# A 12-stage decoder on one core: layer norms' moments taken in the stage before, weight sums and GpSimd fills moved, and another order in the second state-space layer

## The chip, the cores and the metric

The kernel runs on one core of a Trainium2 chip. The metric is the device time of one execution in microseconds (us). Before the change three runs gave a median of 2445.35 us (2441.73 to 2446.42).

## What is computed

The input is `x` of 4 batches x 256 tokens x 256 features in fp32, with a context and two side inputs. The reference is a pre-norm decoder of four layers with three sublayers each:

```python
h = _layernorm(x)                 # mean and variance over the 256 features, eps 1e-5
x = x + sublayer(h)               # twelve times, each with another sublayer
```

The sublayers that the text speaks of, with the short names that the kernel's tiles carry:

- l1a: causal attention with an output bias; m1a and m1b: a Mamba layer (input product, convolution over 4 tokens, SiLU, a product down to 40 rows, a product from 8 of them up again, softplus, then the scan); l1f: a linear layer with ternary weights, added to `x`
- l2a: rotary attention; l2x: experts with quantised weights; l2f: a router keeps the 128 best of 256 tokens of a batch, and only these get the output of a two-layer GELU network
- l3s to l3e: a state-space layer of 16 blocks of 128 channels whose output passes a layer norm with `gamma` and `beta` and then `W_out`; l3xa: cross attention with positions and an output bias; l3f: top-4 of 8 experts

Inside the third layer's state-space part, `layernorm(y) * gamma + beta` times `W_out` is computed as `y @ (gamma * W_out)`, minus the mean times the column sums of `gamma * W_out`, plus the column sums of `beta * W_out`.

## The kernel before

The 1024 tokens lie in 8 tiles of 128 (`NT = 8`, two tiles of one batch, `ST = 2`). The residual `res`, the normed `xn` and its transpose `xT` stay in SBUF for the whole kernel. A stage is a `Stage` block; its exit is a barrier of all engines. In a stage each engine runs its own program in written order, and semaphores alone tie the engines to one another.

Every sublayer but the first begins with `normalize` (tiles `ln_*`; ln4 is the norm ahead of sublayer 4, m1a). It is a `Stage` of its own. SyncE starts the sublayer's weight loads and waits for them. VectorE takes `bn_stats` of eight tiles (L237), `bn_aggr` of them (L241), adds eps (L249, "guess"), refines with a Newton step what ScalarE's Ln and Exp give (L254, L260, L266), makes `shift` (L272) and two normed tiles of each half (L277); ScalarE makes the other four. TensorE transposes, VectorE (L308, L310) and ScalarE (L338, L340) copy to `xT`. ScalarE loads the Exp/Ln table set at the stage's start (L324). GpSimd fills `rowsL` and `rowsR` with ones in ln9 (L320, `ones_in`).

- `attend` (l1a, l2a, l3xa) goes head by head through 4 batches. TensorE's scores `pA` (L1601) wait until VectorE has reduced an earlier `pA` to its maxima (`maximum`, L1734). Four heads make a quad, which VectorE divides by its sum (L1742, L1744). Once a batch, `residual(u)` adds the projected output to `res` (L1779, or L1781 and L1782 with a bias).
- m1a works on two halves of the tokens. `conv`, `silu` (L2031) and the scan's inputs are VectorE's; TensorE makes `pd` (40 rows, L1957) and, from ScalarE's copy of it (`xd`, L1993), the delta product (L1962); ScalarE makes the sigmoids (L1987) and the softplus in four passes (L1997 to L2006).
- l1f: TensorE's products are added by VectorE, a tile at a time (L2242).
- l2x: GpSimd adds the first batches' outputs to `res`; VectorE unscales each (L2644) and adds the last.
- l2f: TensorE makes the up products (L2355), ScalarE the GELU, and the down products (L2366, tile by tile, three PSUM buffers, each freed by VectorE's L2410). VectorE adds the bias (L2410) and the kept tokens to `res` (L2413). It also prepares l3: `scale_and_sum` scales a row block of `W_out` by `gamma` and adds up the sums (L2314, L2316, L2318): 16 blocks, eight of them ahead of the down products and two ahead of each of the first four tiles.
- l3s (`mamba3_ends` with `end=None`) makes the first inputs (`px`, L3175) and from the sums the constants `gw` (two products, a copy L3232). l3e is its counterpart at the end (`start=None`): VectorE adds `gw` to `res` (L3209) and then waits for TensorE's out projection (L3212).

## Time and profile before

| | |
|---|---|
| median of 3 runs | 2445.35 us |
| profiled execution, its own time | 2442.86 us |
| its span | 2441.0 us |
| mean granted TensorE clock | 0.864 of 2.4 GHz |
| busy: TensorE, VectorE, ScalarE, GpSimd | 81%, 72%, 55%, 17% |

The span is the time between the first and the last recorded instruction. Durations of the rows below are from this one execution. An engine's busy share is a mean over twelve sublayers with different limits, so a change in one of them is read from the rows there.

### The profile page before, as it was taken

How to read it: one execution, taken by the hardware profiler on the slowest of the kernel's cores; microseconds unless marked ns; L12 is line 12 of the kernel's file. 1: busy time of each engine (PE TensorE's matmuls, PEld its weight loads, DVE VectorE, ACT ScalarE, POOL GpSimd, SP SyncE). 2: the span in 40 equal slices, each digit the busy share in tenths (PEclk: the TensorE clock that was granted, in tenths of full speed). 3: DMA queues.
4: the chain of work that ended last, by engine and by line, in shares of the span. 5: the costliest groups of instructions: out<-in, count | busy, mean ns of one | idle time of the engine just before them, and what ended most of it. 6: DMA issues, size and time to landing. Idle time of an engine off the chain costs nothing. (4 is left out here: it accounts for less than half of the span.)

```text
span 2441.0 us, 34752 instructions
## 1 busy us (share of the span) xinstructions
PE 1988.1 (81%) x11321; PEld 1310.9 (54%) x11337; DVE 1754.3 (72%) x3900; ACT 1345.1 (55%) x2646; POOL 420.7 (17%) x585
## 2 busy tenths in 40 slices
PE   6999999987666666766877895597999999958978
PEld 4776767764333333543654353455766676733545
DVE  6878888777999998647785874674736373568734
ACT  5777777766989896254334365423323333352641
POOL 2333333322111110003532000201101010110000
PEclk8999999997877777786787798598999999976989
DMA  5000000002111102304202100150000000042010
GB/s 222 3 2 2 3 3 2 1 1 99 58 59 59 40 1 66 114 9 86 54 2 75 51 3 18 49 201 2 1 2 0 2 0 2 1 115 70 16 37 18
DMA packets 62030, 94.52 MB, mean 39 GB/s; under 512 B 9403, under 2 KB 48139, under 8 KB 59415
## 3 DMA queue, kind: packets, MB, share of 16 engines
q1 hardware_dynamic: 58604, 87.81, 11.4%
q0 software_dynamic: 1728, 4.22, 0.8%
q8 instruction: 82, 1.34, 0.2%
q10 hardware_dynamic: 1536, 0.49, 0.1%
q14 instruction: 80, 0.66, 0.1%
HBM read 80.53 MB, written 10.49 MB: 37 GB/s over the span
## 5 line engine op out<-in xcount | busy, mean ns | idle before, releaser
L1260 DVE SCALAR_TENSOR_TENSOR moe_acc<-moee_eo,moe_wsel,moe_acc 128x256 f32<-128x256 bf16 x512 | 226.0, 512 | 0.6
L867 DVE SCALAR_TENSOR_TENSOR l_acc<-l_px,l0w_chan,l_acc 128x253 f32<-128x253 f32 (+2 forms) x288 | 137.6, 478 | 80.6 <-POOL l_acc L835 80.1
L1192 ACT CAST moee_eo<-moee_po 128x512 bf16<-128x512 f32 x256 | 132.5, 596 | 38.5 <-PE moee_po L1165 33.8
L1165 PE MATMUL moee_po<-moee_db,moee_hb 96*128 96x256 bf16 (+1 forms) x768 | 126.9, 329 | 26.1 <-ACT moee_eo L1192 15.5
L1150 PE MATMUL moee_pu<-moe_xb,moee_wb 128*128 128x512 bf16 x192 | 73.1, 522 | 83.4 <-DVE moee_ub L1249 83.4
L1165 PEld LDWEIGHTS moee_po<-moee_db,moee_hb 96*128 96x128 bf16 (+1 forms) x768 | 87.6, 116 | 73.0 <-ACT moee_eo L1192 20.9
L1704 ACT ACTIVATE l3xa_ex<-l3xa_pS 128x512 f32<-128x512 f32 x128 | 74.2, 606 | 81.1 <-PE l3xa_pS L1617 76.7
L1704 ACT ACTIVATE l2a_ex<-l2a_pS 128x512 f32<-128x512 f32 x128 | 73.8, 606 | 76.7 <-PE l2a_pS L1617 72.2
L540 PE MATMUL l_pz<-xT,l0w_w_in 128*128 128x256 f32 x384 | 111.4, 414 | 2.5 <-DVE l_sz L915 2.5
L351 PE MATMUL ln_pt<-ident,xn 128*128 128x128 f32 x176 | 39.6, 418 | 85.9 <-DVE xn L277 85.9
L540 PE MATMUL l_px<-xT,l0w_w_in 128*128 128x256 f32 x384 | 103.5, 394 | 4.3 <-DVE l_acc L867 4.3
L3052 ACT COPY l3b_bc<-l3b_pbc 128x512 f32<-128x512 f32 x48 | 28.1, 586 | 136.4 <-PE l3b_pbc L3002 136.4
L2124 ACT ACTIVATE m1b_dA<-m1w_delta,m1w_a 128x255 f32<-128x255 f32 x128 | 53.3, 462 | 85.8 <-DVE m1b_h L2165 83.4
L652 PE MATMUL l_po<-l0w_w_out,l_yg 128*128 128x256 f32 x384 | 100.4, 385 | 0.0
L3002 PE MATMUL l3b_pbc<-l3w_xin,l3w_w_in 128*128 128x256 f32 x384 | 95.7, 393 | 5.3 <-PEq L72 5.3
L1734 DVE TENSOR_REDUCE l3xa_negm<-l3xa_pA 128x2 f32<-128x512 f32 x128 | 83.1, 684 | 22.8 <-PE l3xa_pA L1601 21.0
L1734 DVE TENSOR_REDUCE l2a_negm<-l2a_pA 128x2 f32<-128x512 f32 x128 | 82.9, 684 | 21.6 <-PE l2a_pA L1601 19.8
L698 ACT ACTIVATE l_acc<-l_px,l0w_chan 128x256 f32<-128x256 f32 x96 | 54.0, 563 | 78.7 <-PE l_px L540 78.5
L852 POOL TENSOR_TENSOR l_ssum<-l_ssum,l_sq 128x256 f32<-128x256 f32 x92 | 68.1, 741 | 148.0 <-ACT l_sq L742 148.0
L2214 PE MATMUL m1b_py<-m1b_hc,ident 128*128 128x256 f32 x256 | 77.3, 466 | 20.1 <-DVE m1b_y L2149 11.4
L903 DVE TENSOR_TENSOR l_gg<-l_dec,l_m 128x768 f32<-128x768 f32 x96 | 91.5, 953 | 0.2
L2135 POOL TENSOR_TENSOR m1b_dBu<-m1w_du,m1b_bc 128x1024 f32<-128x1024 f32 x32 | 75.2, 2354 | 93.9 <-DVE m1b_h L2165 51.9
(614 smaller groups left out, 5508.3 us busy)
## 6 DMA issues: line engine op xcount, KB each, us to landing
moe_wf<-in_moe_up SPq DMA_DIRECT2D x48, 256.0 KB, 2.8
l3w_w_in<-in_l_w_in SPq DMA_DIRECT2D x1, 8224.0 KB, 25.9
m1b_bc<-bc_rows SPq DMA_DIRECT2D x16, 512.0 KB, 10.4
moe_df<-in_moe_down SPq DMA_DIRECT2D x48, 128.0 KB, 3.2
l_qs<-parts_q SPq DMA_DIRECT2D x36, 128.0 KB
l0w_w_in<-in_l_w_in SPq DMA_DIRECT2D x2, 1536.0 KB, 12.7
l0w_w_out<-in_l_w_out SPq DMA_DIRECT2D x1, 3072.0 KB
parts_q<-l_pieces SPq DMA_DIRECT2D x16, 192.0 KB, 2.3
```

What stands on the lines that cost most here:

```text
L540: last = nc.tensor.matmul(out, w_in[:, k, c0:c0 + w], xT[:, k, b, :], start=(k == 0), stop=(k == KT - 1))
L652: last = nc.tensor.matmul(po[:, t * D:(t + 1) * D], yg[:, u % RY, t * P:(t + 1) * P], w_out[:, j, :], start=(j == 0 and t == 0), stop=(j = ...
L867: nc.vector.scalar_tensor_tensor(out=a, in0=px[:, 0:S - (L0_CONV - 1 - c)], scalar=w, in1=a, op0=ALU.mult, op1=ALU.add).then_inc(tap_done, 1)
L903: nc.vector.tensor_tensor(gg[:, :, :], dec[:, v % 2, :, :], m3[:, bv % 2, None, :].broadcast_to([P, 2, SC]), ALU.mult).then_inc(gg_done, 1)
L1165: last = nc.tensor.matmul(po[:, t, :], hb[rows, j % H, t * P:(t + 1) * P], db[rows, j % H, :], start=(n == 0), stop=(n == len(parts) - 1))
L1192: nc.scalar.copy(eo[:, e % 2, 2 * q:2 * q + 2, :], po[:, 2 * q:2 * q + 2, :]).then_inc(o_read, 1)
L1260: last = nc.vector.scalar_tensor_tensor(out=acc[:, t, :], in0=eo[:, e % 2, t, :], scalar=wsel[:, t, e:e + 1], in1=acc[:, t, :], op0=ALU.mu ...
L1704: nc.scalar.activation(ex[:, at % XR, :, :], pS[:, at % 2, :, :], ACT.Exp, scale=scale).then_inc(exp_done, 1)
L1734: nc.vector.tensor_reduce(negm[:, u % 2, t, 2 * pair:2 * pair + 2], pA[:, at % 2, :, 0:keys(t)], AX, ALU.max, negate=True).then_inc(maxed, 1)
L2135: nc.gpsimd.tensor_tensor(dBu[:, i % R, :, :], du[:, n, None, b * S:(b + 1) * S].broadcast_to([P, CH, S]), bc[:, b % 2, c * CH:(c + 1) * C ...
L2214: last = nc.tensor.matmul(py[:, n, :], g["ident"][:, :], hc[:, i % R, q, :], start=(c == 0 and n == 0 and q == 0), stop=(c == NCH - 1 and ...
L3002: last = nc.tensor.matmul(pbc[:, n * S:(n + 1) * S], w_in[:, k, c0 + j * P:c0 + (j + 1) * P], xin[:, k, :], start=(k == 0), stop=(k == KT ...
```

## The change

It has five parts.

1. `stats` and `mv` are tiles of the whole kernel. `moments_ahead` takes the moments of some tiles in the stage before the norm, on VectorE, as soon as their residual is final: 6 tiles for ln4, ln6, ln7, ln9, ln10 and ln11, 4 for ln8; ln1, ln2, ln3 and ln5 are as before. `normalize(..., ahead=n)` begins with "guess" of the first half and takes the moments of what is left. Its table load moves to the end of ScalarE's program of the stage before (for ln8 and ln10 it goes, as that set is loaded there).
2. `scale_and_sum` runs once per tile in l2f (blocks 0 to 7, none ahead of the tiles), and blocks 8 to 15 in l3s, where the two `gw` products move behind the `px` products.
3. GpSimd's two fills move from ln9 to the start of l2f.
4. m1a: on VectorE `silu(0)` stands ahead of `conv(1, 0)`; on ScalarE the first half's sigmoids stand ahead of the gate's, its `copy_xd(0)` ahead of the second half's sigmoids, and its first softplus ahead of `copy_xd(1)`.
5. The waits that go with these (`added`, `summed`, `out_chain`, `early_added`, `sums_done`).

```diff
-def normalize(nc, g, loads=(), early=None, ones_in=(), mix=None):
+def moments_ahead(nc, g, link, tiles):
+
+    for t in tiles:
+        last = nc.vector.bn_stats(g["stats"][:, t, :], g["res"][:, t, :])
+    link(last)
+    for t in tiles:
+        nc.vector.bn_aggr(g["mv"][:, t, :], g["stats"][:, t, :])
+
...
-                for t in range(H):
-                    stat(t)
-                stat(4)
-                for t in range(H):
-                    aggregate(t)
-                stat(5)
-                guess(0)
-                stat(6)
-                stat(7)
-                newton_a(0)
-                aggregate(4)
-                aggregate(5)
-                newton_b(0)
-                aggregate(6)
-                aggregate(7)
+                if ahead:
+                    guess(0)
+                    for t in range(ahead, NT):
+                        stat(t)
+                    newton_a(0)
+                    for t in range(ahead, NT - 1):
+                        aggregate(t)
+                    newton_b(0)
+                    aggregate(NT - 1)
+                else:
...
-                nc.scalar.preload_act_table_set(EXP_LN)
+                if not ahead:
+                    nc.scalar.preload_act_table_set(EXP_LN)
...
                         nc.scalar.copy(oT[:, :, :], pE[:, :].rearrange("p (k q) -> p k q", k=KT)).then_inc(oT_done, 1)
+                nc.scalar.preload_act_table_set(EXP_LN)
...
-                        residual(batch_at(j, ADD_AT))
+                        u = batch_at(j, ADD_AT)
+                        residual(u)
+                        if u < B - 1:
+                            dve.wait_ge(added, u + 1)
+                            moments_ahead(nc, g, link, range(ST * u, ST * (u + 1)))
...
                     nc.scalar.activation(gate[:, :, :], xn[:, :, :], ACT.Sigmoid).then_inc(gate_sig, 1)
-                    for half in range(2):
-                        for n in range(M1_ET):
-                            act.wait_ge(conv_done, M1_ET * half + n + 1)
-                            nc.scalar.activation(sig[:, n, tokens(half)], u[:, n, tokens(half)],
-                                                 ACT.Sigmoid).then_inc(sig_done, 1)
+                    copy_xd(0)
+                    sigmoid(1, 0)
+                    sigmoid(1, 1)
                     nc.scalar.preload_act_table_set(EXP_LN)
                     nc.scalar.activation(a[:, :, :], a[:, :, :], ACT.Exp).then_inc(exp_done, 1)
-                    for half in range(2):
-                        act.wait_ge(xd_proj, half + 1)
-                        nc.scalar.copy(xd[:, tokens(half)], pd[0:M1_R + 2 * M1_N, half, :]).then_inc(xd_done, 1)
...
+                    softplus(0, 0)
+                    copy_xd(1)
+                    softplus(0, 1)
+                    softplus(1, 0)
+                    softplus(1, 1)
...
                     conv(0, 0)
                     conv(0, 1)
+                    silu(0)
                     conv(1, 0)
-                    silu(0)
                     conv(1, 1)
                     silu(1)
...
                     for t in range(NT):
+                        if 1 <= t < NT - 1:
+                            dve.wait_ge(summed, t)
+                            moments_ahead(nc, g, link, (t - 1,))
                         dve.wait_ge(added, t + 1)
                         dve.wait_ge(outp, t + 1)
                         nc.vector.tensor_tensor(res[:, t, :], res[:, t, :], po[:, t % 4, 0:D], ALU.add).then_inc(summed, 1)
+
+                @block.scalar
+                def _(act):
+                    nc.scalar.preload_act_table_set(EXP_LN)
...
+                @block.gpsimd
+                def _(pool):
+                    for rows in ahead["rows"]:
+                        nc.gpsimd.memset(rows[:, :, :], 1.0)
...
+                    nc.scalar.preload_act_table_set(EXP_LN)
...
-                    for j in range(L3_J // 2):
-                        scale_and_sum(dve, link, j)
                     dve.wait_ge(second_in, 32)
                     for t in range(NT):
-                        for j in range(L3_J // 2 + 2 * t, min(L3_J // 2 + 2 * t + 2, L3_J)):
-                            scale_and_sum(dve, link, j)
+                        if t == 0:
+                            dve.wait_ge(ahead["out_in"], 32)
+                        scale_and_sum(nc, link, ahead, t)
+                        if 1 <= t < NT - 1:
+                            dve.wait_ge(out_chain, t)
+                            moments_ahead(nc, g, link, (t - 1,))
                         dve.wait_ge(down, t + 1)
...
                     unscale(6)
+                    dve.wait_ge(early_added, 2)
+                    moments_ahead(nc, g, link, range(0, 2 * ST))
                     unscale(7)
...
+        half_tokens(nc, g, {"w_in": w_in, "w_out": w_out, "chan": chan, "sums": sums, "w_in_in": w_in_in,
+                            "out_in": out_in, "rows": (rowsL, rowsR)})
         g["stage"] = 9
-        normalize(nc, g, early=(w_in_in, 16), ones_in=(rowsL, rowsR))
+        normalize(nc, g, early=(w_in_in, 16), ahead=6)
...
+                if end is None:
+                    pe.wait_ge(sums_done, 1)
+                    for n in range(2):
+                        last = nc.tensor.matmul(po[:, n, 0:D], g["ones"][:, 0:P], m["sums"][:, n, :], start=True,
+                                                stop=True)
+                    last.then_inc(gw_ready, 1)
...
                         link(nc.vector.tensor_tensor(now, now, gw[:, 1, :], ALU.add))
+                    if start is None:
+                        moments_ahead(nc, g, link, range(NT - ST))
                     dve.wait_ge(used, ST)
...
                 if end is None:
+                    for j in range(NT, L3_J - 1):
+                        scale_and_sum(nc, link, m, j)
+                    row = w_out[:, L3_J - 1, 0:D]
+                    link(nc.vector.scalar_tensor_tensor(out=m["sums"][:, 1, :], in0=row,
+                                                        scalar=m["chan"][:, L3_J - 1, 2:3], in1=m["sums"][:, 1, :],
+                                                        op0=ALU.mult, op1=ALU.add))
+                    link(nc.vector.tensor_scalar(row, row, m["chan"][:, L3_J - 1, 1:2], None, ALU.mult))
+                    nc.vector.tensor_tensor(m["sums"][:, 0, :], m["sums"][:, 0, :], row, ALU.add).then_inc(sums_done, 1)
                     dve.wait_ge(gw_ready, 1)
                     nc.vector.tensor_copy(gw[:, :, :], po[:, :, 0:D])
```

On VectorE in l2f, at the down products' second tile (`l2f_po` is their PSUM, `l3w_w_out` and `l3w_sums` are `W_out` and its sums for l3), before:

```order
L2410 TENSOR_TENSOR l2f_tmp<-l2f_po,l2fw_b 128x256
L2413 SCALAR_TENSOR_TENSOR res<-l2f_tmp,l2f_keep,res 128x256
L2314 SCALAR_TENSOR_TENSOR l3w_sums<-l3w_w_out,l3w_chan,l3w_sums 128x256
L2316 TENSOR_SCALAR l3w_w_out<-l3w_w_out,l3w_chan 128x256
L2318 TENSOR_TENSOR l3w_sums<-l3w_sums,l3w_w_out 128x256
L2314 SCALAR_TENSOR_TENSOR l3w_sums<-l3w_w_out,l3w_chan,l3w_sums 128x256
L2316 TENSOR_SCALAR l3w_w_out<-l3w_w_out,l3w_chan 128x256
L2318 TENSOR_TENSOR l3w_sums<-l3w_sums,l3w_w_out 128x256
L2410 TENSOR_TENSOR l2f_tmp<-l2f_po,l2fw_b 128x256
L2413 SCALAR_TENSOR_TENSOR res<-l2f_tmp,l2f_keep,res 128x256
```

and after:

```order
L2464 TENSOR_TENSOR l2f_tmp<-l2f_po,l2fw_b 128x256
L2467 SCALAR_TENSOR_TENSOR res<-l2f_tmp,l2f_keep,res 128x256
L2322 SCALAR_TENSOR_TENSOR l3w_sums<-l3w_w_out,l3w_chan,l3w_sums 128x256
L2324 TENSOR_SCALAR l3w_w_out<-l3w_w_out,l3w_chan 128x256
L2326 TENSOR_TENSOR l3w_sums<-l3w_w_out 128x256
L208 BN_STATS stats<-res 128x6
L211 BN_AGGR mv<-stats 128x2
L2464 TENSOR_TENSOR l2f_tmp<-l2f_po,l2fw_b 128x256
L2467 SCALAR_TENSOR_TENSOR res<-l2f_tmp,l2f_keep,res 128x256
```

One block of `W_out` stands ahead of the tile where two stood, and the moments of the tile before have come in.

On ScalarE at the middle of m1a (`m1a_sig` the sigmoids of two pieces a half, `m1w_gate` that of the gate, `m1w_xd` the copy of the 40 rows), before:

```order
L1980 COPY m1a_raw<-m1a_px 128x2x256 x4
L1983 ACT_TABLE_LOAD
L1983 ACTIVATE m1w_gate<-xn 128x2048
L1987 ACTIVATE m1a_sig<-m1w_u 128x512 x4
L1989 ACT_TABLE_LOAD
L1990 ACTIVATE m1w_a<-m1w_a 128x32
L1993 COPY m1w_xd<-m1a_pd 40x512
L1997 ACTIVATE m1a_soft<-m1a_px,m1w_chan 128x512
```

and after:

```order
L2006 COPY m1a_raw<-m1a_px 128x2x256 x4
L2012 ACT_TABLE_LOAD
L2012 ACTIVATE m1a_sig<-m1w_u 128x512 x2
L2036 ACTIVATE m1w_gate<-xn 128x2048
L2017 COPY m1w_xd<-m1a_pd 40x512
L2012 ACTIVATE m1a_sig<-m1w_u 128x512 x2
L2040 ACT_TABLE_LOAD
L2041 ACTIVATE m1w_a<-m1w_a 128x32
L2022 ACTIVATE m1a_soft<-m1a_px,m1w_chan 128x512
```

The first `m1w_xd` has moved ahead of two sigmoids, the table load and `m1w_a`.

On VectorE in l2a at the residual of the first batch (`l2a_pA` scores, `l2a_negm` their maxima), before:

```order
L1734 TENSOR_REDUCE l2a_negm<-l2a_pA 128x2 x3
L1779 TENSOR_TENSOR res<-res,l2a_pE 128x256 x2
L1734 TENSOR_REDUCE l2a_negm<-l2a_pA 128x2
L1742 RECIPROCAL l2a_rden<-l2a_pX 128x8
L1744 TENSOR_TENSOR l2a_o<-l2a_pX,l2a_rden 128x32 x2
```

and after:

```order
L1755 TENSOR_REDUCE l2a_negm<-l2a_pA 128x2 x3
L1800 TENSOR_TENSOR res<-res,l2a_pE 128x256 x2
L208 BN_STATS stats<-res 128x6 x2
L211 BN_AGGR mv<-stats 128x2 x2
L1755 TENSOR_REDUCE l2a_negm<-l2a_pA 128x2
L1763 RECIPROCAL l2a_rden<-l2a_pX 128x8
L1765 TENSOR_TENSOR l2a_o<-l2a_pX,l2a_rden 128x32 x2
```

Four operations stand between the add and the next reduction of scores.

## Rows read from the trace of the kernel before

**Rows 1.** The page: TensorE's granted clock in 40 slices of the span.

```profile
PEclk8999999997877777786787798598999999976989
```

**Rows 2.** Timeline of VectorE in ln7: start, us, then line, names, idle before.

```profile
1498.02 1.73 DVE L237 BATCH_NORM_STATS2 ln_stats<-res 128x6 f32<-128x256 f32 x5 [1.28 <-PEq L72]
...
1500.26 0.15 DVE L249 TENSOR_SCALAR ln_var<-ln_mv 128x4 f32<-128x4 f32 x1
...
1505.92 0.42 DVE L310 COPY xT<-ln_pt 128x256 f32<-128x256 f32 x1
```

**Rows 3.** SyncE's queue in ln7: what it waited for, us, times, longest.

```profile
SPq L222 <- PEq L222: 3.3, 1, 3.3
```

**Rows 4.** SyncE's queue in ln11, the same columns.

```profile
SPq L222 <- PEq L222: 0.2, 1, 0.2
```

**Rows 5.** Timeline of VectorE in ln9.

```profile
1660.11 2.40 DVE L249 TENSOR_SCALAR ln_var<-ln_mv 128x4 f32<-128x4 f32 x1
...
1666.64 0.41 DVE L310 COPY xT<-ln_pt 128x256 f32<-128x256 f32 x1
```

**Rows 6.** Timeline of GpSimd in ln9.

```profile
1655.51 3.50 POOL L320 MEMSET l3w_rowsL<- 38x4096 bf16 x1 [88.27 <-POOLq L72]
1658.96 3.52 POOL L320 MEMSET l3w_rowsR<- 38x4096 bf16 x1
```

**Rows 7.** Timeline of VectorE, its first operation in l2f.

```profile
1588.06 0.23 DVE L2386 TENSOR_SCALAR l2f_score<-l2f_ps,l2fw_b_r 128x8 f32<-128x8 f32 x1 [7.79 <-PE l2f_ps L2344]
```

**Rows 8.** Timeline of TensorE in l2f: where the down products resume.

```profile
1633.11 1.22 PE L2366 MATMUL l2f_po<-l2fw_w,l2f_hT 128*128 128x256 f32 x2 [4.54 <-DVE l2f_tmp L2410]
```

**Rows 9.** Timeline of VectorE in l2f's down products.

```profile
1631.26 0.48 DVE L2314 SCALAR_TENSOR_TENSOR l3w_sums<-l3w_w_out,l3w_chan,l3w_sums 128x256 f32<-128x256 f32 x1
...
1632.63 0.42 DVE L2410 TENSOR_TENSOR l2f_tmp<-l2f_po,l2fw_b 128x256 f32<-128x256 f32 x1
...
1649.93 0.42 DVE L2410 TENSOR_TENSOR l2f_tmp<-l2f_po,l2fw_b 128x256 f32<-128x256 f32 x1 [2.51 <-PE l2f_po L2366]
...
1653.39 0.42 DVE L2410 TENSOR_TENSOR l2f_tmp<-l2f_po,l2fw_b 128x256 f32<-128x256 f32 x1 [2.51 <-PE l2f_po L2366]
```

**Rows 10.** l2f in stretches: us, busy of each engine, granted clock, DMA share.

```profile
1633.10:1638.60 5.50, 5.49 (x13) 4.41 (x14) 5.15 (x13) 0.00 (x0) 0.00 (x0) 0.50 0.01 3
```

**Rows 11.** Timeline of TensorE in l3s.

```profile
1671.40 14.58 PE L3175 MATMUL l3s_px<-l3w_w_in,l3w_xin 128*128 128x512 f32 x32
```

**Rows 12.** Timeline of VectorE in m1a, the second half's first convolution.

```profile
1097.67 2.33 DVE L2020 SCALAR_TENSOR_TENSOR m1w_u<-m1a_raw,m1w_chan,m1w_u 128x512 f32<-128x512 f32 x3
```

**Rows 13.** Timeline of TensorE in m1a.

```profile
1101.25 3.63 PE L1957 MATMUL m1a_pd<-m1w_u,m1w_w_x 128*40 128x512 f32 x4 [7.02 <-DVE m1w_u L2031]
1106.74 3.78 PE L1962 MATMUL m1a_px<-m1w_xd,m1w_w_dt 8*128 8x512 f32 x4 [1.86 <-ACT m1w_xd L1993]
```

**Rows 14.** Timeline of ScalarE in m1a.

```profile
1114.12 0.58 ACT L1993 COPY m1w_xd<-m1a_pd 40x512 f32<-40x512 f32 x1
1116.86 0.69 ACT L1997 ACTIVATE m1a_soft<-m1a_px,m1w_chan 128x512 f32<-128x512 f32 x1 [2.16 <-PE m1a_px L1962]
...
1121.46 0.63 ACT L2006 ACTIVATE m1a_soft<-m1a_soft 128x512 f32<-128x512 f32 x1
```

**Rows 15.** Timeline of VectorE in l2a, at the first residual add.

```profile
1411.76 0.74 DVE L1779 TENSOR_TENSOR res<-res,l2a_pE 128x256 f32<-128x256 f32 x2
```

**Rows 16.** Timeline of TensorE in l2a behind that add.

```profile
1414.19 0.39 PE L1601 MATMUL l2a_pA<-l_ks,l_qs 96*128 96x256 bf16 x2
```

**Rows 17.** Timeline of TensorE in l3xa behind the first residual add.

```profile
2272.77 0.39 PE L1601 MATMUL l3xa_pA<-l3x_ks,l3x_qs 96*128 96x256 bf16 x2 [0.54 <-DVE l3xa_negm L1734]
```

**Rows 18.** Timeline of VectorE in l1f's adds.

```profile
1291.62 0.42 DVE L2242 TENSOR_TENSOR res<-res,l1f_po 128x256 f32<-128x256 f32 x1 [0.44 <-PE l1f_po L2255]
```

**Rows 19.** Timeline of VectorE in l2x, the last tile.

```profile
1568.85 0.88 DVE L2644 SCALAR_TENSOR_TENSOR l2x_h<-l2x_po,l2x_rows,l2x_wrow 128x256 f32<-128x256 f32 x2 [2.96 <-PE l2x_po L2867]
```

**Rows 20.** Timeline of VectorE in l3e.

```profile
2139.51 0.16 DVE L3212 TENSOR_SCALAR l3e_small<-l3e_po 128x2 f32<-128x2 f32 x1 [15.40 <-PE l3e_pq L3162]
```

More of the change, by code:

```diff
@@ L239, in aggregate @@
                 def aggregate(t):
-                    dve.wait_ge(stats_done, t + 1)
+                    dve.wait_ge(stats_done, t + 1 - ahead)
                     nc.vector.bn_aggr(mv[:, t, :], stats[:, t, :]).then_inc(moments, 1)
@@ L246, in guess @@
                 def guess(h):
-                    dve.wait_ge(moments, (h + 1) * H)
+                    if (h + 1) * H > ahead:
+                        dve.wait_ge(moments, (h + 1) * H - ahead)
                     nc.vector.tensor_scalar(var[:, half(h)], mv[:, half(h), 1], LN_EPS, None,
@@ L278, in scaled @@
                                             ALU.subtract, ALU.mult).then_inc(xn_v, 1)
-                for t in range(H):
-                    stat(t)
-                stat(4)
-                for t in range(H):
-                    aggregate(t)
-                stat(5)
-                guess(0)
-                stat(6)
-                stat(7)
-                newton_a(0)
-                aggregate(4)
-                aggregate(5)
-                newton_b(0)
-                aggregate(6)
-                aggregate(7)
+                if ahead:
[8 more added lines that the diff above has]
+                else:
+                    for t in range(H):
+                        stat(t)
+                    stat(4)
+                    for t in range(H):
+                        aggregate(t)
+                    stat(5)
+                    guess(0)
+                    stat(6)
+                    stat(7)
+                    newton_a(0)
+                    aggregate(4)
+                    aggregate(5)
+                    newton_b(0)
+                    aggregate(6)
+                    aggregate(7)
                 newton_c(0)
@@ L1853, in positional_cross @@
         vaug = st.sbuf("vaug", [P, NT, H, HD + 1])
-        normalize(nc, g, [(w[:, :, :, :], I["l3x_w"]), (wk[:, :, :, :], I["l3x_wk"]), (rows[:, :], I["l3x_row"])])
+        normalize(nc, g, [(w[:, :, :, :], I["l3x_w"]), (wk[:, :, :, :], I["l3x_wk"]), (rows[:, :], I["l3x_row"])],
+                  ahead=6)
         stacks = head_stacks(st, H, H)
@@ new lines, in copy_xd, with softplus @@
+                    def copy_xd(half):
+                        act.wait_ge(xd_proj, half + 1)
+                        nc.scalar.copy(xd[:, tokens(half)], pd[0:M1_R + 2 * M1_N, half, :]).then_inc(xd_done, 1)
+                    def softplus(half, n):
+                        i = M1_ET * half + n
+                        act.wait_ge(dt_proj, i + 1)
+                        nc.scalar.activation(soft[:, 0, n, tokens(half)], px[:, n, half, :],
+                                             ACT.Identity, bias=chan[:, n, 5:6]).then_inc(a_chain, 1)
+                        act.wait_ge(a_chain, 3 * i + 1)
+                        nc.scalar.activation(soft[:, 1, n, tokens(half)], soft[:, 0, n, tokens(half)],
+                                             ACT.Abs).then_inc(a_chain, 1)
+                        act.wait_ge(a_chain, 3 * i + 2)
+                        nc.scalar.activation(soft[:, 2, n, tokens(half)], soft[:, 1, n, tokens(half)], ACT.Exp,
+                                             scale=-1.0).then_inc(a_chain, 1)
+                        act.wait_ge(a_chain, 3 * i + 3)
+                        nc.scalar.activation(soft[:, 3, n, tokens(half)], soft[:, 2, n, tokens(half)], ACT.Ln,
+                                             bias=1.0).then_inc(soft_done, 1)
@@ L2264, with scale_and_sum @@
 MOD_KEEP = S // 2
+def scale_and_sum(nc, link, m, j):
+    w_out, sums, gamma, beta = m["w_out"], m["sums"], m["chan"][:, j, 1:2], m["chan"][:, j, 2:3]
+    row = w_out[:, j, 0:D]
+    if j == 0:
+        nc.vector.memset(w_out[:, :, D:D + 1], 1.0)
+        link(nc.vector.tensor_scalar(sums[:, 1, :], row, beta, None, ALU.mult))
+        link(nc.vector.tensor_scalar(row, row, gamma, None, ALU.mult))
+        return
+    link(nc.vector.scalar_tensor_tensor(out=sums[:, 1, :], in0=row, scalar=beta, in1=sums[:, 1, :],
+                                        op0=ALU.mult, op1=ALU.add))
+    link(nc.vector.tensor_scalar(row, row, gamma, None, ALU.mult))
+    before = w_out[:, 0, 0:D] if j == 1 else sums[:, 0, :]
+    link(nc.vector.tensor_tensor(sums[:, 0, :], before, row, ALU.add))
 def half_tokens(nc, g, ahead):
@@ L2294, in half_tokens @@
             rope = g["xn"][:, :, :].rearrange("p (n t) d -> p n (t d)", n=2)
[L2295 removed]
+            w_out, chan = ahead["w_out"], ahead["chan"]
             ph = st.psum("ph", [P, 4, 512])
@@ L2545, in quant_experts @@
         wgu = wst.sbuf("wgu", [P, KT, B, S])
-        normalize(nc, g, [(wgu[:, :, :, :], I["l2x_gu"])])
+        normalize(nc, g, [(wgu[:, :, :, :], I["l2x_gu"])], ahead=6)
         with Stage(nc, "l2x") as st:
@@ L3163, in _ @@
                                          start=True, stop=True).then_inc(used, 1)
-                if end is None:
-                    for n in range(2):
-                        last = nc.tensor.matmul(po[:, n, 0:D], g["ones"][:, 0:P], m["sums"][:, n, :], start=True,
-                                                stop=True)
-                    last.then_inc(gw_ready, 1)
                 if start is not None:
```

63 lines of the change are left out of this document (21 added, 42 removed).

## The prediction

> **What bounds the kernel now.** The page comes first: TensorE is busy for 81% of the span, and its clock line [rows 1] stays below 9 over long stretches, so the stages have different limits. The change touches four kinds of places, so each is read from its own timeline, not from the shares. In a norm nothing else runs, and the path is a chain: VectorE's moments, the guess, ScalarE's Ln and Exp, Newton, the normed tiles, transposes, copies. In ln7 the statistics start at 1498.02, the guess comes at 1500.26, the last copy ends at 1506.34: 8.32 us [rows 2]. The other chain there is SyncE's, the weight loads; its queue's waits tell which of the two ends a norm. In ln7 SyncE waits 3.3 us for TensorE after its load has landed, so compute decides [rows 3]; in ln11 it waits only 0.2 us, so there the 2 MB of expert weights decide nearly as much [rows 4]. In l2f's down products TensorE stood idle for 4.54 us until VectorE had freed a buffer at L2410 [rows 8]. In m1a the engines hand one value back and forth, and TensorE waits 7.02 us for `silu` and 1.86 us for a copy on ScalarE [rows 13]. In l2a TensorE is paced by its own work, with VectorE just behind it [rows 15, 16].
>
> **The norms.** The moments of six tiles leave each of ln4, ln6, ln7, ln9, ln10, so the guess is the first operation: 1500.26 - 1498.02 = 2.24 us earlier [rows 2]. What follows keeps its spacing, since only two `bn_stats` (five took 1.73, so 0.35 each) still stand behind the guess and ScalarE needs about as long. I take 2.24 for each, 11.2 in all. Bounds: nothing, where SyncE ends the norm, and 2.24. SyncE's slack in ln7 is 3.3 [rows 3], and I take the others as ln7, their loads being of its kind; ln9 has no load. ln11 can give only its slack of 0.2 [rows 4]. ln8 has four tiles left, two more `bn_stats` between guess and Newton: 2.24 - 0.7 = 1.5. Sum: -12.9. The table load that went to the end of the stage before costs nothing there: ScalarE's last copies end ahead of VectorE's last adds, and if one didn't, a load would cost less than the 2.24 us of moments under which it lay in the norm.
>
> **The fills.** In ln9 the second L249 takes 2.40 us where such an operation takes 0.15 [rows 2, 5]; it ends at 1662.51, when the second fill has ended at 1658.96 + 3.52 = 1662.48 [rows 6]. From the first fill's start to VectorE's last copy the norm takes 1667.05 - 1655.51 = 11.5 us, in ln7 8.3 [rows 2, 5, 6]. So without the fills it gains 3.2: -3.2 (bounds 0 and 3.3). In l2f they lie where VectorE waits 7.79 us for the router's products, until 1588.06 [rows 7]; the fills take 7.02 [rows 6] from the stage's start, so they just fit: 0, at worst a few tenths. The Trainium skill (SBUF — State Buffer, "Who interferes with whom") says that VectorE and GpSimd share one pair of ports as an exclusive lock, and that a `tensor_scalar` in a two-port mode waits for a whole GpSimd instruction; by that rule the gain is the whole remainder of each fill, as the trace shows. The page would also let the fills hold l2f's first VectorE operations if they came later than that idle time.
>
> **l2f's down products.** Before, eight blocks of `W_out` and two more ahead of the first tile stand in front of VectorE's first L2410, which comes at 1632.63; a block takes 1632.63 - 1631.26 = 1.37 us [rows 9]. TensorE had filled its three buffers by 1633.11 - 4.54 = 1628.57, waited, and then ran at half clock for 5.5 us [rows 8, 10]; the last product ended at 1653.35 [rows 9]. Afterwards VectorE needs per tile 1.37 for a block, 0.5 for the moments (0.35 plus the aggregation) and 0.9 for the two old operations, 2.8 us, less than the 3.46 us that TensorE takes for a tile (1653.39 - 1649.93 [rows 9]). So TensorE isn't held: the remaining five tiles follow 1628.57 directly and end at 1628.57 + 5 x 3.46 = 1645.9. That is -7.5: 4.5 of idle time and 3 of half clock. Bounds: -4.5, if the clock falls there anyway; none, if `W_out` landed late, but its blocks were being worked on long before.
>
> l3s gets eight blocks, 8 x 1.37 = 11 us, under the 14.58 us of `px` [rows 11]. The two `gw` products move from in front of `px` to behind it, which is neutral, and the copy of `gw` now follows at the very end, where ScalarE's copy of the last `px` ended before: +0.2 (0 to 0.7).
>
> **m1a.** Before: `pd` of the first half starts at 1101.25 and takes 3.63, its copy waits on ScalarE behind a sigmoid and the table load, and the delta product starts at 1106.74 and ends at 1110.5 [rows 13]; then `pd` of the second half (another 3.6), its copy at 1114.12, the delta product, and two softplus from 1116.86 to 1122.09, 2.62 each [rows 14]. Afterwards `silu(0)` comes one `conv` (three passes in 2.33 us and a first one, together some 2.8 [rows 12]) earlier: it is done at about 1098.6, `pd` ends 1102.3, the copy (0.58) follows at once, the delta product ends 1106.7, the second `pd` 1110.4, its copy 1111.0. ScalarE has done one softplus by then, and three remain: 1111.0 + 3 x 2.62 = 1118.9 against 1122.09. So -3.0 (0.2 held back for hand-overs). Bounds: -4 if the clock opens earlier, -1 if the gate's sigmoid gets in front of the copy.
>
> **What it costs: attention.** Six tiles' moments stand in `attend` at u = 0, 1, 2 in l1a, l2a and l3xa: two `bn_stats` 0.7, a wait, two aggregations, 1.04 us in front of the next reduction (an estimate from [rows 2]). What is late next is that reduction, and then TensorE's `pA`. In l2a the `pA` product at 1414.19 starts as soon as the reduction behind the add (1411.76) and its followers allow [rows 15, 16]; in l3xa TensorE already waits 0.54 there [rows 17]. So the delay passes through whole at u = 0 and 1: 4 x 1.04 = 4.1. At u = 2 VectorE has idle time ahead of its next work, 0 to 0.3. l1a's quads are shorter on VectorE, and I take 1.0, 0.6 and 0.35: 2.0. Sum +6.1, bounds 0 and 9 x 1.04 = 9.4.
>
> The other moments are covered. l1f: the block (0.5) is a little longer than VectorE's wait of 0.44 per tile [rows 18]; that drifts for five tiles, and the last tile, with no block ahead of it, takes it back: +0.1 (without that, 0.5). l2x: four tiles, 1.8 us, in a wait of 2.96 [rows 19]. l3e: six tiles in 15.40 [rows 20].
>
> **The sum.** -12.9 - 3.2 - 7.5 - 3.0 + 6.1 + 0.2 + 0.1 = -20.2 us. Against the profiled execution's own 2442.86 us (span 2441.0 and 1.9 around it) that is 2422.7; the runs' median 2445.35 lies 2.5 above that execution, so 2425.2.
>
> **Rivals.** A measurement of this kernel tells about 0.2%, 4.9 us, from no change.
> - Attention pays nothing, since later slack takes the delays back: -26, 2419. For it: TensorE's path in l1a has waits of its own. Against: [rows 16, 17].
> - l2f gives only its idle time, because VectorE's chain or the late half clock paces it: 3 to 5 us less, 2429. Against: 2.8 under 3.46.
> - Attention pays double: each late reduction also delays ScalarE's exponentials and the next quad, or u = 2 costs as much: +6 more, 2431.
> - Slower: the stalls bring down TensorE's clock. After l2f's 4.54 us of idle time the clock was 0.50 for 5.5 us [rows 8, 10], which costs 2.75. If each of the nine stalls in attention did that: +24.8, 2450, slower than before. It decides from the point where a stall of 1 us is enough and does it at all nine. Against: the waits of l3xa [rows 17] leave the clock line at 9 in the slice that holds them (2258 to 2319) [rows 1]. [...]
> - The change doesn't shorten the norms: the loads, or ScalarE's table, end them, as in ln11. Then 12.7 of the gain are gone: -7.5, 2438, and with any further loss no change. Against: [rows 3].
>
> **Chances.** My forecast, -16 to -24, 0.65; attention free 0.10; l2f small 0.10; attention double 0.07; norms unchanged 0.05, of which half within 0.2%; slower by the clock 0.03. Faster 0.94, same 0.03, slower 0.03. The range leaves out the last two and the ends of the first: 2417 to 2434.
>
> **What would show it.** Right: in ln4, ln6, ln7, ln9, ln10 the guess first on VectorE and the norm 2.2 us shorter; ln9's L258 at 0.15; ln11 about as long as before, with SyncE's last wait for TensorE near 0; no idle time of TensorE over 1 us in l2f's down products, and a full clock there; m1a's last softplus ending 3 us sooner after the barrier ahead of m1a; behind each residual of l2a and l3xa at u = 0, 1 a wait of TensorE for `negm` of about 1 us. Wrong: norms that end on SyncE, a clock of 0.5 in attention, or a VectorE that waits at l2f's start for the fills.

## The result and the profile after

The changed kernel takes 2424.76 us (median of 4 runs, 2420.86 to 2426.5) against 2445.89 us for the kernel before with its runs of the same day (4 runs, 2441.73 to 2446.63). The ratio is 0.9917, its 95% interval 0.9901 to 0.9932, that is 16.6 to 24.2 us less. The forecast was 2425.2 us, within 2417 to 2434. The profiled execution has a span of 2419.0 us, 22.0 less than before. In the timelines below a line's columns are its start and duration in us, the engine, the line of kernel.py, the operation, the tiles written and read, their shapes, how many were merged, and in brackets the idle time before it with what ended it.

Norm ln7 on VectorE after the change, which answers to [rows 2]:

```profile
1493.04 0.17 DVE L258 TENSOR_SCALAR ln_var<-mv 128x4 f32<-128x4 f32 x1 [1.28 <-PEq L72]
1493.12 0.75 DVE L245 BATCH_NORM_STATS2 stats<-res 128x6 f32<-128x256 f32 x2
...
1498.81 0.42 DVE L329 COPY xT<-ln_pt 128x256 f32<-128x256 f32 x1
```

The guess comes first and the last copy ends 6.19 us after it, where it ended 8.32 us after the first statistics. In ln9, which answers to [rows 5], the second guess takes 0.17 and not 2.40 us, and the norm 6.31 us in all:

```profile
1637.73 0.17 DVE L258 TENSOR_SCALAR ln_var<-mv 128x4 f32<-128x4 f32 x1 [1.22 <-PEq L72]
...
1638.94 0.17 DVE L258 TENSOR_SCALAR ln_var<-mv 128x4 f32<-128x4 f32 x1
...
1643.62 0.42 DVE L329 COPY xT<-ln_pt 128x256 f32<-128x256 f32 x1 [0.16 <-PE ln_pt L371]
```

SyncE's queue in ln11 (what it waited for, total us, times, longest) says what it said in [rows 4]: the load ends the norm, and SyncE then waits only 0.2 us for TensorE:

```profile
SPq L230 <- DMA l3fw_w<-in_l3f_w: 7.0, 1, 7.0
...
SPq L230 <- PEq L230: 0.2, 1, 0.2
```

In l2f the fills lie where [rows 7] had the wait (first GpSimd, then VectorE); VectorE's first operation starts 1.3 us before the second fill ends (1579.02):

```profile
1572.06 3.50 POOL L2419 MEMSET l3w_rowsL<- 38x4096 bf16 x1 [12.04 <-POOLq L72]
1575.51 3.51 POOL L2419 MEMSET l3w_rowsR<- 38x4096 bf16 x1
```

```profile
1577.73 0.23 DVE L2438 TENSOR_SCALAR l2f_score<-l2f_ps,l2fw_b_r 128x8 f32<-128x8 f32 x1 [6.43 <-PE l2f_ps L2390]
```

Its matrix operand lies in PSUM and has 8 columns, and it wasn't held. The down products, which answer to [rows 8], are one group of 128 without a wait:

```profile
1607.57 27.89 PE L2412 MATMUL l2f_po<-l2fw_w,l2f_hT 128*128 128x256 f32 x128 [0.78 <-ACT l2f_hT L2426]
```

TensorE in m1a, for [rows 13]: the copy comes at once (0.67 and not 1.86 us of waiting), and ScalarE's last softplus ends 28.96 us after the stage's first operation, where it ended 33.46 us after it:

```profile
1098.00 2.54 PE L1983 MATMUL m1a_pd<-m1w_u,m1w_w_x 128*40 128x512 f32 x4 [4.16 <-DVE m1w_u L2070]
1101.21 3.78 PE L1988 MATMUL m1a_px<-m1w_xd,m1w_w_dt 8*128 8x512 f32 x4 [0.67 <-ACT m1w_xd L2017]
1105.03 3.64 PE L1983 MATMUL m1a_pd<-m1w_u,m1w_w_x 128*40 128x512 f32 x4
1109.33 1.99 PE L1988 MATMUL m1a_px<-m1w_xd,m1w_w_dt 8*128 8x512 f32 x4 [0.67 <-ACT m1w_xd L2017]
```

What it costs shows in l2a at the first residual, on VectorE and on TensorE [rows 15, 16]:

```profile
1404.71 0.74 DVE L1800 TENSOR_TENSOR res<-res,l2a_pE 128x256 f32<-128x256 f32 x2
1405.49 0.75 DVE L208 BATCH_NORM_STATS2 stats<-res 128x6 f32<-128x256 f32 x2
1406.28 0.25 DVE L211 BATCH_NORM_AGGREGATE mv<-stats 128x2 f32<-128x6 f32 x2
1406.44 0.66 DVE L1755 TENSOR_REDUCE l2a_negm<-l2a_pA 128x2 f32<-128x512 f32 x1
```

```profile
1407.16 0.39 PE L1621 MATMUL l2a_pA<-l_ks,l_qs 96*128 96x256 bf16 x2 [0.67 <-DVE l2a_negm L1755]
...
1408.19 0.39 PE L1621 MATMUL l2a_pA<-l_ks,l_qs 96*128 96x256 bf16 x2 [0.42 <-DVE l2a_negm L1755]
```

The reduction starts 1.73 us after the add did, where it started 0.66 after it (1412.42 against 1411.76), so a block costs 1.07; TensorE waits 0.67 and 0.42, together the same 1.09.

### The profile page after: what moved, and what is told of

Same layout as the page of the kernel before. It is cut to its first block and busy times, and to the rows that moved or that the text cites. A ratio compares the mean times of both kernels' runs of the same rounds, so it can differ in the third digit from the quotient of the medians.

```text
span 2419.0 us, 34769 instructions
## 1 busy us (share of the span) xinstructions
PE 1999.5 (83%) x11337; PEld 1312.5 (54%) x11337; DVE 1755.9 (73%) x3900; ACT 1344.7 (56%) x2644; POOL 421.3 (17%) x585
## 5 line engine op out<-in xcount | busy, mean ns | idle before, releaser
L1185 PE MATMUL moee_po<-moee_db,moee_hb 96*128 96x256 bf16 (+1 forms) x768 | 134.9, 343 | 28.4 <-ACT moee_eo L1212 21.0
L1212 ACT CAST moee_eo<-moee_po 128x512 bf16<-128x512 f32 x256 | 133.1, 595 | 38.3 <-PE moee_po L1185 35.5
L3131 POOL TENSOR_TENSOR l3w_yz<-l3b_ys,l3b_sz 128x256 f32<-128x256 f32 x48 | 40.1, 836 | 290.7 <-DVE l3b_ys L3160 290.7
```

The source lines that it names most:

```text
L1185: last = nc.tensor.matmul(po[:, t, :], hb[rows, j % H, t * P:(t + 1) * P], db[rows, j % H, :], start=(n == 0), stop=(n == len(parts) - 1))
L1212: nc.scalar.copy(eo[:, e % 2, 2 * q:2 * q + 2, :], po[:, 2 * q:2 * q + 2, :]).then_inc(o_read, 1)
```

## The experiments

There were eleven runs: the changed kernel and the kernel before once more, and nine variants. The medians of the kernel before lie between 2442.5 and 2446.0 us from run to run and its single executions up to 14 us apart, so the tables below go by stages of the profiled executions: a stage's length is from the first operation behind its opening barrier to the first one behind the next, read from the timelines. For attention TensorE's busy time in that window is given too. What is left, length less busy time, is its waiting, and that repeats within 0.1 us in kernels that share the code of l2a. The scatter lies in the busy time, which holds what the clock costs.

**Another execution of each kernel.**

> The changed kernel once more, for how far stages that no edit touches differ between executions. My theory: stages outside the change, and the pieces at half clock within it (the start of l2f, m1a's two pd products), move by 1 to 3 us from execution to execution, so that of m1a's 4.5 us measured only 3 are the edit's and of l2f's 8.9 only 7.5. Then m1a lasts 31.2 to 32.7 us here and l2f 65.7 to 67. Rival: the edits give the whole 4.5 and 8.9; then this execution repeats 31.2 and 65.7 within 0.1. Total 2421 to 2427 us by both.

2424.62 us (4 runs, 2422.23 to 2432.56), ratio 0.992 (0.9904 to 0.9935); but the profiled execution has a span of 2430.2, 11 us above the first. m1a took 31.16 and l2f 67.10. So of l2f's 8.8 us between the first two profiles 1.4 were scatter, and m1a's length repeated: the first theory holds for l2f, the rival for m1a as far as this run goes.

> The kernel before once more, for its stages. If m1a's 35.7 us in the first profile is a matter of where the clock stood, it takes 32.7 here, as in the three kernels that leave m1a alone; rival: it is the usual length, 35.7 again. l2f 73.2 to 74.5, ln9 12.3, l2a 157.7 to 158.6 by both.

2449.37 us (one execution). m1a took 34.62, l2f 73.21, ln9 12.31, l2a 158.52. m1a's 35.7 was neither the usual length nor a single case.

**The weight sums alone.** Edit: part 2 of the change in the kernel before, no moments moved.

```diff
-                    for j in range(L3_J // 2):
-                        scale_and_sum(dve, link, j)
...
                     for t in range(NT):
-                        for j in range(L3_J // 2 + 2 * t, min(L3_J // 2 + 2 * t + 2, L3_J)):
-                            scale_and_sum(dve, link, j)
...
+                        scale_and_sum(nc, link, ahead, t)
```

> The kernel before with the weight sums' move alone: one block per tile in l2f, eight in l3s, the gw products behind px; no moments moved. My theory: TensorE's idle time of 4.54 us and its 5.5 us at half clock both go, so l2f lasts 74.5 - 7.5 = 67.0 us (66 to 68 with the clock's scatter in its first products), and the kernel 7.3 us less than before. Rival: the half clock comes anyway (from where it falls in the run): l2f 70, kernel 4.3 less.

l2f took 67.03 us, l3s 19.85 (as before). Ratio 0.9965 (0.9945 to 0.9985), median 2434.25. The first theory.

**The same with the eight blocks ahead of the down products.**

```diff
                     for j in range(L3_J // 2):
-                        scale_and_sum(dve, link, j)
+                        scale_and_sum(nc, link, ahead, j)
...
                     for t in range(NT):
-                        for j in range(L3_J // 2 + 2 * t, min(L3_J // 2 + 2 * t + 2, L3_J)):
-                            scale_and_sum(dve, link, j)
```

> As the weight sums' move alone, but the eight blocks of l2f all stand ahead of the down products, as before. VectorE reaches the first bias add at about 1630.4 - not 1632.6 - so TensorE idles some 1.9 us and not 4.54. This asks what a shorter wait does to the clock. My theory (the half clock follows the long idle time): with 1.9 us of idle time no half clock, l2f 74.5 - 2.7 - 2.75 = 69 us. Rival, any wait of TensorE brings the half clock: l2f 71.8 us with a stretch of 0.50 behind the wait.

l2f took 69.06 us; ratio 0.9968 (0.9952 to 0.9983), median 2439.09. TensorE's timeline and the stretch behind the wait (length, busy of each engine, granted clock 1.00):

```profile
1628.53 11.71 PE L2366 MATMUL l2f_po<-l2fw_w,l2f_hT 128*128 128x256 f32 x53 [1.80 <-DVE l2f_tmp L2409]
```

```profile
1628.50:1634.00 5.50, 5.47 (x25) 4.85 (x26) 3.03 (x7) 0.00 (x0) 0.00 (x0) 1.00 0.04 13
```

The first theory. A wait of 1.80 us left the clock at 1.00 (2.4 GHz) here, one of 4.54 us was followed by 0.50 (1.2 GHz) [rows 8, 10], in all four executions profiled with it. So what l2f gains is the wait and its consequence, and the two don't shrink together: shortening the wait to 1.80 removed the half clock whole.

**m1a's order alone.** Edit: part 4 of the change in the kernel before.

> The kernel before with m1a's new order alone. My theory: m1a goes from 35.7 to 32.7 us with the clock where it was, and down to 31.2 where the first pd product meets the higher clock (it took 2.54 us and not 3.63 in the changed kernel). Rival: the whole 4.5 us is the order's; then 31.2 whatever that product takes. The kernel as a whole 3 us less than before.

m1a took 31.37 us. Ratio 0.9969 (0.9949 to 0.9988), median 2438.97. All lengths of m1a, over every profile:

| m1a | executions | us |
|---|---|---|
| order of before | 5 | 35.71, 34.62, 32.72, 32.73, 32.72 (mean 33.7) |
| order of after | 8 | 31.21, 31.16, 31.24, 31.26, 31.37, 30.23, 30.27, 30.26 (mean 30.9) |

The two groups don't overlap, and their means are 2.8 apart. Neither side of the expectation was right as put: the length is the order's and the clock's. Against the three executions of 32.7, the three of 30.2 are 2.5 less.

**The fills alone.** Edit: part 3 in the kernel before.

> The kernel before with GpSimd's two fills in l2f and no longer in ln9. My theory: they held VectorE in ln9; ln9 goes from 12.3 to 9.1 us (start to the next stage's first copy), l2f keeps 74.5, and the kernel is 3.2 us less. Rival: VectorE was slow there for another cause, as GpSimd's start or the weights' arrival: ln9 keeps over 11 us.

ln9 took 9.38 us and not 12.31, l2f 73.19. Ratio 0.9996 (0.9985 to 1.0008): 2.9 us in one stage aren't told from nothing by whole runs, the stage shows them.

**Attention without the moments.** ln4, ln7 and ln11 take all eight tiles themselves and load their table set themselves:

```diff
                         residual(u)
-                        if u < B - 1:
-                            dve.wait_ge(added, u + 1)
-                            moments_ahead(nc, g, link, range(ST * u, ST * (u + 1)))
```

> The changed kernel without the moments in attention: ln4, ln7 and ln11 take all eight tiles' moments themselves, with their table load. My theory: attention's blocks cost what the profile after shows, 2.9 us in l1a, 2.1 in l2a, 2.2 in l3xa, and the three norms give back 2.2, 2.1 and nothing; so this kernel is 2.8 us faster than the changed one (about 2422), l2a lasts 157.7 us and not 159.8, l3xa 161.1 and not 163.3, l1a 95.7 and not 98.6. Rival: attention's lengths differ for other causes (clock); then l2a and l3xa keep 159.8 and 163.3 and the kernel is 4.3 us slower than the changed one.

2423.85 us (6 runs), ratio 0.9919 (0.9905 to 0.9934): 0.8 less than the changed kernel where 2.8 was expected; whole runs tell neither of the two from nothing. l1a 93.53, l2a 160.40, l3xa 162.70, ln4 and ln7 9.37 and 9.32. By its length alone l2a would speak for the rival; the table below shows that its waiting is back at 19.06 and that the rest is 2.7 us of busy time. The clock stood at 0.50 for the stage's first 38.6 us, where it did for 35.6 with the changed kernel, and for 3.4 us more near its end.

**The moments in one block.** The same six tiles, but ahead of the last residual, where VectorE waits for the out projection:

```diff
+                        if u == B - 1:
+                            dve.wait_ge(added, B - 1)
+                            moments_ahead(nc, g, link, range(ST * (B - 1)))
                         residual(u)
-                        if u < B - 1:
-                            dve.wait_ge(added, u + 1)
-                            moments_ahead(nc, g, link, range(ST * u, ST * (u + 1)))
```

> The changed kernel with the six tiles' moments of each attention in one block ahead of the last residual, where VectorE waits 3.3 us or more for the out projection; a block of six takes about 2.9 us. My theory: a block costs only where VectorE is late next, so here nothing: l2a 157.7, l3xa 161.1, l1a 95.5 to 96; ln4 and ln7 stay at 7.1 and 7.0 us; the kernel is 6 to 7 us faster than the changed one, about 2418. Rival: the block doesn't fit and delays the last add by up to 2 us in each of the three; then 0 to 2 us faster than the changed one.

2417.4 us (6 runs, 2414.25 to 2423.8), ratio 0.9899 (0.9883 to 0.9915). l1a 95.39, l2a 158.63, l3xa 161.11, ln4 7.07, ln7 6.95. The first theory: in l2a VectorE waited 3.42 us ahead of the last add in the kernel before and 0.91 here. Not all of the 7.3 us that this kernel is faster by the medians is the block's, though: l3xp, the projections ahead of l3xa, which this edit doesn't touch, took 41.7 us here and in the kernel with both improvements, and 43.5 to 45.2 in the eleven other executions. TensorE's clock was 1.00 in its first 4 us in these two, and 0.50 for the first 3.4 us or more in the others. Why isn't known.

**The blocks doubled.**

```diff
                             moments_ahead(nc, g, link, range(ST * u, ST * (u + 1)))
+                            n = NT * ("l1a", "l2a", "l3xa").index(name)
+                            for t in range(ST * u, ST * (u + 1)):
+                                last = nc.vector.bn_stats(g["stats2"][:, n + t, :], g["res"][:, t, :])
+                            link(last)
+                            for t in range(ST * u, ST * (u + 1)):
+                                nc.vector.bn_aggr(g["mv2"][:, n + t, :], g["stats2"][:, n + t, :])
...
```

> The changed kernel with each of attention's nine blocks of moments taken twice (the second into tiles that nobody reads), so that VectorE comes 2.1 us late and not 1.04. It asks from which length a stall brings TensorE's clock down. Theory A, the delays add and the clock stays: l2a 161.9, l3xa 165.4, l1a some 101, the kernel 7 us slower than the changed one. Theory B, a stall of 2 us in attention is followed by a stretch at half clock, as already now and then in l1a with 1.04: stretches of 0.50 behind most blocks at u = 0 and 1, each 2 us more, the kernel 12 to 20 us slower.

2437.29 us (10 runs), ratio 0.9963 (0.995 to 0.9976), 12.7 us above the changed kernel. All of attention, length less TensorE's busy time:

| kernel | l1a | l2a | l3xa |
|---|---|---|---|
| before | 95.39 - 80.72 = 14.67 | 157.71 - 138.65 = 19.06 | 161.10 - 139.38 = 21.72 |
| before, again | 96.54 - 81.92 = 14.62 | 158.52 - 139.50 = 19.02 | 163.40 - 140.79 = 22.61 |
| no moments | 93.53 - 79.52 = 14.01 | 160.40 - 141.34 = 19.06 | 162.70 - 140.46 = 22.24 |
| one late block | 95.39 - 81.38 = 14.01 | 158.63 - 139.58 = 19.05 | 161.11 - 138.65 = 22.46 |
| after | 98.60 - 82.70 = 15.90 | 159.80 - 138.66 = 21.14 | 163.31 - 139.23 = 24.08 |
| after, again | 99.88 - 83.33 = 16.55 | 160.78 - 139.65 = 21.13 | 165.36 - 141.27 = 24.09 |
| blocks doubled | 104.19 - 85.69 = 18.50 | 162.45 - 139.22 = 23.23 | 168.70 - 141.86 = 26.84 |

The waiting grows by 2.1 us with the blocks in l2a, by 4.2 with doubled ones, and by nothing with one late block. In l1a the busy time grows as well. In all thirteen executions each of the three stages begins at 0.50, for 23 to 27 us in l1a and 36 to 39 in l2a and l3xa; what follows is about falls behind that. In the doubled kernel, at l1a's first residual (TensorE's timeline, then stretches with the granted clock as the number behind the five engines):

```profile
1033.36 0.23 PE L1621 MATMUL l1a_pA<-l_ks,l_qs 96*128 96x128 bf16 x1 [2.17 <-DVE l1a_negm L1755]
```

```profile
1031.00:1034.00 3.00, 0.83 (x12) 0.51 (x9) 2.86 (x14) 0.99 (x5) 0.00 (x0) 1.00 0.00 0
1034.00:1037.00 3.00, 2.52 (x19) 1.88 (x22) 1.71 (x6) 0.41 (x2) 0.00 (x0) 0.50 0.05 11
1037.00:1040.00 3.00, 3.00 (x29) 1.91 (x29) 1.44 (x5) 1.40 (x6) 0.00 (x0) 0.50 0.02 3
1040.00:1043.00 3.00, 3.00 (x40) 2.29 (x38) 2.37 (x5) 1.66 (x6) 0.00 (x0) 0.87 0.00 0
```

So theory B is right in l1a (falls at u = 0, at u = 1 and near the end) and in l3xa (two short ones, behind waits of 2.50 us at u = 0 and 1), theory A in l2a, where the waits were 1.58 us and the clock stayed at 1.00 from the end of the opening stretch on:

```profile
1375.50:1500.10 124.60, 107.27 (x1030) 59.03 (x1022) 77.54 (x225) 78.93 (x160) 0.64 (x2) 1.00 0.01 3
```

**l3f's second weights from l3f's own block.**

```diff
-        normalize(nc, g, [(wg[:, :, :], I["l3f_wg"]), (earlier[:, :, :], I["earlier"]), (w1[:, :, :], I["l3f_w1"]),
-                          (w2[:, :, :], I["l3f_w2"])], ahead=6)
+        normalize(nc, g, [(wg[:, :, :], I["l3f_wg"]), (earlier[:, :, :], I["earlier"]), (w1[:, :, :], I["l3f_w1"])],
+                  ahead=6)
...
+                @block.sync
+                def _(sp):
+                    sp.dma_start(w2[:, :, :], I["l3f_w2"]).then_inc(w2_in, 16)
...
+                            if i == 0:
+                                pe.wait_ge(w2_in, 16)
```

> The changed kernel with l3f's second weights (1 MB) loaded from l3f's own block, waited for ahead of the first down product, and no longer in ln11. My theory: ln11 was as long as before (9.6 us) because the loads end it; without half of them it takes 7.1 us as ln10 does, and the down products find the weights there: 2.3 us faster than the changed kernel, about 2422.5. Rival: ln11 has another bound (ScalarE's table, TensorE's clock): then it stays over 9 us and the kernel is unchanged.

ln11 took 7.24 us and not 9.62; l3f 71.08 (71.62 and 71.05 with the changed kernel). 2422.01 us (4 runs), ratio 0.9912 (0.9896 to 0.9928). SyncE's queue in ln11:

```profile
SPq L230 <- DMA l3fw_w<-in_l3f_w: 4.4, 1, 4.4
SPq L230 <- PEq L230: 0.8, 1, 0.8
```

**Both improvements.**

> The changed kernel with both improvements: attention's six moments in one block ahead of the last residual, and l3f's second weights loaded from l3f's own block. Each gave its part in its own run (attention 6 to 7 us by the stages, ln11 2.3 us). My theory: they add, since they lie in different stages: ln11 7.1 us, l2a 157.7, l3xa 161.1, about 9 us under the changed kernel, 2415 us. Rival: the clock gives a part back; then 5 us under it, 2419.

2413.84 us (5 runs, 2408.78 to 2418.73), ratio to the kernel before 0.988 (0.9859 to 0.9901): 32 us less than its 2446.03 and, by the medians, some 11 less than the changed kernel. ln11 7.25, l1a 93.87, l2a 158.58, l3xa 161.34. This is the fastest kernel of the case.

## Why the prediction was right

The time came out as forecast, and so did the mechanism of the norms, the fills, l2f and m1a. The step that was wrong inside a right forecast is attention's: its clock stood at nothing in the sum. Each term beside what the profiles show; with more than two executions, it is the mean over all with an edit less the mean over all without it, and "from" gives typical ones:

| term | forecast | measured | from |
|---|---|---|---|
| moments out of ln4, ln6, ln7, ln10 | -2.24 each | -2.3, -2.6, -2.2, -2.3 | 9.37 to 7.08, 9.37 to 6.75, 9.14 to 6.97, 9.38 to 7.08 |
| ln8 | -1.5 | -1.8, later -1.6 | 9.38 to 7.55, and 7.80 in six other executions |
| ln9, moments and fills | -2.24 - 3.2 | -5.2 | 12.31 to 7.08; fills alone -2.9 |
| ln11 | -0.2 | +0.4 | mean of 7: 9.47; of 4: 9.84 (9.41 to 9.62 in the first two) |
| l2f | -7.5 | -6.6 | mean of 4: 73.8; of 8: 67.2 |
| m1a | -3.0 | -2.8 | 33.7 to 30.9 |
| attention, VectorE's delay | +6.1 | +5.7 | waiting, means of 7 and 3: l1a +1.6, l2a +2.1, l3xa +2.0 |
| attention, lower clock in l1a | none | +2.1 | busy: mean of 7 without 80.5, of 3 with 82.7 |
| l3s and l1f | +0.3 | 0 | l3s 19.85 to 19.72; ln5 and l1f together 20.32, and 20.25 to 20.36 in five executions without the edit (19.95 in the first) |

The terms measured add up to about -17.5, the forecast had -20.2, and the whole runs say -16.6 to -24.2 with 21.1 between the medians. So it is luck in part that the forecast of 2425.2 lies 0.4 us from the median: l2f gave 0.9 less, attention cost 1.7 more, ln11 lost a little instead of gaining, and 3.6 us between the terms and the medians are in none of them. The difference of the two first profiles, -22.0, holds besides them 2.7 us in the first sublayer, which no edit touches: its main stage took 521.25 and 518.56 us there, and 518.6 to 524.5 over all profiles.

**The norms.** The step "what follows keeps its spacing" held, and SyncE's slack told which norm would gain nothing: ln11. That this was the load and not the table or the clock is shown by the kernel without half of the load, which gained 2.4 there. ln6 gave 2.6 and so more than the forecast's bound of 2.24: 2.2 of it is waiting, 0.4 is TensorE's busy time (3.67 to 3.2), which the sum had left out.

**The fills.** The rows of ln9 had 3.2 for them, alone they gave 2.9. In l2f they "just fit" by the rows of before, and they did where VectorE waited 7.79 us for the router's products; in the profile after and with the fills alone those products ended earlier (waits of 6.43 and 6.24 us), and VectorE's first operation ran beside the second fill without being held. The Trainium skill (SBUF — State Buffer, "Who interferes with whom") lets `tensor_scalar` contend in its two-port modes, when its operands meet their conditions; this operation from PSUM, 128x8, was free, the one in ln9, 128x4 and from SBUF [rows 5], was held. Which property of it decides was not tried.

**l2f.** The step was "TensorE isn't held": it is one group of 128 products. 4.45 of the 6.6 us are waiting (7.53 to 3.08) and the rest, 2.2, is busy time, where the forecast had 3 for the half clock. Behind the wait the clock was the same in all four executions without the edit, 0.50, and in none with it; what differs is the half clock with which the stage begins, 7 to 10 us long without the edit and 7 to 11 with it.

**m1a.** The chain went in the order forecast; the durations hang on the clock. The size was right on the mean, and that is luck in part, since the execution before that it was worked out from was the longest of five. There both delta products (L1962) ran at half clock (3.78 us each), in three others neither did (1.98 to 2.20). The forecast named the clock as its bound (-4), and the first two profiles showed -4.5, beyond it.

**Attention.** The delay passed whole at u = 0 and 1 in l2a and l3xa and not at u = 2. In l1a the term of 2.0 was mis-sized: 1.6 of waiting and 2.1 of busy time, 3.7 in length (95.0 to 98.7). In all three executions with the blocks the clock fell inside l1a, behind u = 0 or u = 1 or both; in the seven executions without them and the two with a late block it fell, after the opening stretch, only near the end or not at all. In l3xa it fell behind u = 1 in one of the three. So the mechanism of the slower rival was there, and with it a sign that the prediction had named for being wrong, "a clock of 0.5 in attention": at 1 or 2 of 9 blocks, in l1a each time and in l3xa once, where the forecast had given it to all or none. Stretches of three us of the changed kernel's l1a, from the first block on, show it:

```profile
1030.33:1033.33 3.00, 1.42 (x20) 1.04 (x17) 2.86 (x12) 1.27 (x5) 0.00 (x0) 1.00 0.00 0
1033.33:1036.33 3.00, 2.86 (x30) 1.83 (x30) 2.38 (x8) 0.79 (x4) 0.00 (x0) 0.66 0.06 14
1036.33:1039.33 3.00, 3.00 (x35) 2.44 (x28) 1.50 (x4) 2.10 (x9) 0.00 (x0) 0.77 0.00 0
```

TensorE is busy 1.42 of 3 us; its wait for `negm`, 0.21 us without the blocks, is now 1.25 at once, and shorter waits stand behind it in both. In the kernel with the weight sums alone the same place reads 2.31 of 3.00 and the clock stays at 1.00:

```profile
1032.97:1035.97 3.00, 2.31 (x31) 1.74 (x32) 2.78 (x10) 1.08 (x5) 0.00 (x0) 1.00 0.03 6
1035.97:1038.97 3.00, 1.87 (x32) 1.37 (x32) 1.41 (x5) 1.59 (x7) 0.00 (x0) 1.00 0.04 8
```

The wait alone doesn't decide it: in the second execution of the changed kernel the same 1.25 us at u = 0 left the clock at 1.00. That execution's fall in l3xa comes behind waits of 1.58 and 0.42 us:

```profile
2294.40:2297.80 3.40, 3.40 (x24) 1.64 (x23) 2.22 (x6) 0.71 (x2) 0.00 (x0) 0.50 0.02 5
```

The Trainium skill (TensorE: Matmul & The Clock Gate, "HAM oscillation — how this bites in real kernels") describes such falls in a kernel whose TensorE waits some 3 to 5 us for a DMA again and again. The rows of l2f agree (4.54 us). The waits of 1.25 to 2.50 us that stood ahead of falls in l1a and l3xa are shorter than its case, and the 1.58 us in l2a, with the blocks doubled, weren't followed by one.

By the stages the net of the moments moved into attention was a loss of 3.3 us: 5.7 of waiting and 2.1 of busy time in l1a against 4.5 gained in ln4 and ln7 and nothing in ln11. Whole runs, 0.8 apart, don't show it. The forecast had both sides of this sum (+6.1 against -4.7) but not the conclusion that the blocks stood at the wrong place. What stays open is why the clock falls in l1a at u = 0 in one execution and at u = 1 in another, and whether l2a is spared by how its work lies or by chance.

## What to carry to other kernels

Work that is taken out of a serial stretch should go where its engine waits for the longest time, not where its data first become final: six tiles' moments at three residuals cost 5.7 us and more in three stages, the same six ahead of the last one nothing in l1a and l2a and at most half a us in l3xa, and the norm gained the same. Before shortening a stage's compute, read the loads that end it: SyncE's last wait (0.2 us in ln11, 3.3 in ln7) told which norms would gain. Where the effect is a few us and whole runs scatter by as much, compare stages of several executions, and TensorE's waiting apart from its busy time.
